# Weighted sums of two key tiles back to back in every second period of an attention pipeline

## The reference

```
attn = einsum('bhld,bhrd->bhlr', q, k) * 0.25
rel  = einsum('bhld,lrd->bhlr', q, dist_emb[clip(r - l, -64, 8) + 64]) * 0.25
attn = softmax(attn + rel, axis=-1)
out  = einsum('bhlr,bhrd->bhld', attn, v)
```

## Time and profile before

| | |
|---|---|
| median of 3 runs | 1690.88 us |
| the profiled execution | 1693.59 us |
| its span | 1691.8 us |
| TensorE matmul busy over the span | 1395.4 us (82%) |
| VectorE busy | 1091.4 us (65%) |
| ScalarE busy | 991.8 us (59%) |
| GpSimd busy | 235.3 us (14%) |

### The profile page before, as it was taken

How to read it: one execution, slowest core, us unless ns; L and a number is a source line. 1 busy time by engine, 2 the same in 40 slices (tenths; PEclk the granted TensorE clock), 3 DMA queues, 4 the chain that set the end, 5 groups by cost and what they waited for, 6 DMA issues and landing times. The chain is left out here.

```text
span 1691.8 us, 25838 instructions
## 1 busy us (share of the span) xinstructions
PE 1395.4 (82%) x8108; PEld 685.2 (41%) x8108; DVE 1091.4 (65%) x2552; ACT 991.8 (59%) x1697; POOL 235.3 (14%) x472
## 2 busy tenths in 40 slices
PE   7851599999999999999999997798995989810487
PEld 4520133444334443344433432566662434300476
DVE  3540888878888788887888870246432329979554
ACT  4530177777777777777777775244443548868600
POOL 0001121212212122121221200113310000000011
PEclk9975599999999999999999998878867999965699
DMA  6859588787887878878788611322202102205022
GB/s 191 237 151 243 167 222 233 198 231 220 223 233 196 231 220 224 233 196 234 216 226 232 176 53 54 111 71 66 61 26 87 37 0 112 112 26 195 27 85 89
DMA packets 263819, 260.03 MB, mean 154 GB/s; under 512 B 65902, under 2 KB 250894, under 8 KB 259598
## 3 DMA queue, kind: packets, MB, share of 16 engines
q1 hardware_dynamic: 263694, 258.49, 53.2%
HBM read 149.30 MB, written 108.35 MB: 152 GB/s over the span
## 5 line engine op out<-in xcount | busy, mean ns | idle before, releaser
L500 ACT ACTIVATE pr<-scoresT 128x512 f32<-128x512 f32 x1024 | 550.5, 600 | 217.3 <-PE scoresT L744 158.9
L740 PE MATMUL scoresT<-qT,kT 99*128 99x512 bf16 (+7 forms) x1408 | 358.9, 326 | 6.7 <-issue 5.0
L609 DVE CUSTOM_DVE_ANT_0 junk<-scores_for_max,win 128x200 f32<-128x200 f32 (+2 forms) x512 | 180.1, 352 | 199.3 <-PE scores_for_max L715 196.7
L614 DVE TENSOR_REDUCE mx<-scores_for_max 128x1 f32<-128x888 f32 (+6 forms) x448 | 301.7, 673 | 0.0
L612 DVE TENSOR_REDUCE mx<-scores_for_max 128x1 f32<-128x64 f32 (+6 forms) x448 | 277.5, 619 | 0.0
L757 PE MATMUL attn_out<-pr,vS 128*17 128x512 f32 x2048 | 269.4, 598 | 0.1
L740 PEld LDWEIGHTS scoresT<-qT,kT 99*128 99x128 bf16 (+1 forms) x1408 | 113.7, 97 | 335.4 <-ACT rows L480 97.8
L744 PE MATMUL scoresT<-idf,win 128*128 128x128 f32 x1024 | 218.2, 274 | 0.0
L714 PE MATMUL scores_for_max<-kX,qT 64*128 64x512 bf16 x512 | 169.7, 394 | 19.4 <-DVE mx L614 18.0
L1741 PE MATMUL banks<-w_downT,work 128*128 128x256 f32 x384 | 88.5, 395 | 105.8 <-DVE work L1712 105.8
L715 PE MATMUL scores_for_max<-kX,qX 64*128 64x512 bf16 x512 | 169.8, 394 | 0.0
(11 more groups left out here) (161 smaller groups left out, 1691.9 us busy)
## 6 DMA issues: line engine op xcount, KB each, us to landing
rel_table<-rows SPq DMA_DIRECT2D x128, 512.0 KB, 4.1
win<-rel_table SPq DMA_DIRECT2D x128, 512.0 KB, 5.3
up_raw<-ub SPq DMA_DIRECT2D x6, 1536.0 KB, 5.1
ub<-up_raw SPq DMA_DIRECT2D x6, 1536.0 KB, 6.3
qT<-q_parts SPq DMA_DIRECT2D x32, 256.0 KB, 7.4
kX<-k_parts SPq DMA_DIRECT2D x64, 128.0 KB, 4.9
kT<-k_parts SPq DMA_DIRECT2D x32, 256.0 KB, 5.4
q_parts<-part SPq DMA_DIRECT2D x32, 192.0 KB, 4.3
```

The costliest lines, as they stand in the source:

```text
L500: nc.scalar.activation(pr[:, n % NPR, h, :], bank, ACT.Exp).then_inc(t_read, 1)
L609: last = nc.vector.tensor_tensor_reduce(junk[:, n % 2, 0:z - a], bank[:, a:z], win[:, T % NW, q4, h, u:u + z - a], 1.0, NEG, ALU.add, ALU. ...
L614: last = nc.vector.tensor_reduce(mx[:, T % 2, q4, h, 2:3], bank[:, z:L], AX.X, ALU.max)
L740: last = mm(bank[:, a:e], k[0:r], q[0:r, a:e], start=(n == 0), stop=not near and n == len(pieces) - 1, skip_group_check=True)
```

## The change

In place of one `weigh` in each period, TensorE does none in odd periods and two in even ones: those of the two key tiles before. Nothing else is moved, no buffer is added, and no other engine's program changes.

```
                     if kt == SHIFT_AT and T + 1 < NT:
                         turn_shift(T + 1)
-                    if kt:
+                    if kt and kt % 2 == 0:
+                        weigh(T, kt - 2)
                         weigh(T, kt - 1)
-                    elif T:
+                    elif kt == 0 and T:
+                        weigh(T - 1, TL - 2)
                         weigh(T - 1, TL - 1)
+            weigh(NT - 1, TL - 2)
             weigh(NT - 1, TL - 1)
             turn_out(NT - 1)
```

## The result

The change makes the kernel slower. Its median is 1747.2 us (4 runs, 1741.05 to 1756.81), against 1691.98 us for the kernel before on the same chip (4 runs). The ratio is 1.0326, with a 95% interval of 1.0265 to 1.0388. The forecast was 1752 us, range 1739 to 1773, with TensorE held up by VectorE's chunk buffers.

A forecast was written before the change was run, and what follows sets the result against it. TensorE was taken to be held up by VectorE's two-deep chunk buffers: 121 pairs at 0.51 us, 61.9, less 1.2 for the last 6, gave +60.7 us. On 1690.9 that is 1752 us, range 1739 to 1773.

The forecast's parts named there:

- The floor: Two-deep chunk buffers: VectorE allows no less than 3.24 us from one period's first chunk to the next's second, 3.11 outer.
- odd stretches: From an odd period's first chunk to the even period's second; six at 3.24 and two at 3.11, 25.66 us.
- The pair: Two `weigh` in a row in each even period; the second was taken to add 0.88 us, its passes alone.
- The saved changes: TensorE's switches between `weigh` and other matmuls; a pair of periods was to have 0.20 us less work.
- The rival of two full changes: The second `weigh` still pays both changes, 1.08 us in place of 0.88; 1777 us in all, chance 0.08.
- The sum: Sixteen periods: odd and even parts together 56.99 us against 52.90, so 4.09 us more for 8 pairs, 0.51 a pair.
- even stretches: From an even period's second chunk to the next odd first chunk; eight grow by 0.88 each, 24.29 to 31.33 us.
- VectorE recovers part: Waits in even periods vanish as VectorE and ScalarE catch up; loss 12 us smaller, 1740, within the forecast's 0.75.
- The last pairs: The 6 pairs at the end, after the chunks stop, only gain 0.20 us each: -1.2 us.
- the two dearer rivals: Two `weigh` in a row paying both changes, 1777 us, and ScalarE later by 0.2 us a pair, 1776; chances 0.08 and 0.06.
- narrowly in period 1: ScalarE's three score banks let the second chunk come at 2.6 or 3.1 us, hidden under VectorE's 3.24.
- a third chunk buffer: Would make true the rival that TensorE alone sets the pace: 25 us faster, 1666, chance 0.05.

The follow-up runs named there:

- pairs_act: The changed kernel with ScalarE's exponentials covering 256 of 512 queries from the fourth period on; median 1738.83 us, against 1682.36 us for the order of before with this cut.
- pairs_dve: The changed kernel with each VectorE maximum reduction beside the window reading at most 64 columns; median 1678.09 us.
- single_dve: The kernel before, its order kept, with each VectorE maximum reduction beside the window reading at most 64 columns; median 1664.24 us.
- pairs_both: The changed kernel with VectorE's reductions at most 64 columns wide and half of ScalarE's exponentials left out from the fourth period on; median 1642.3 us.

## Why the prediction was right

**The floor.** Forecast 3.24 us between an odd period's first chunk and the next second chunk, and 3.11 in outer query tiles; measured 3.24 and 3.11 in 118 of 121 odd stretches. Cutting VectorE's work took seven tenths of the loss away (61.2 to 17.6 us), and cutting ScalarE's too turned the rest into a gain of 5.7 us, which shows that this is the cause and not only a coincidence of numbers.

**The pair.** Forecast 0.88 us for the second `weigh`, measured 0.87 in the stretch shown. The saved changes are 1.43 us per 16 periods; eight times 0.20, 1.6, was the estimate. The rival of two full changes is refuted by the pass starts. The prediction said that the trace of before has no two in a row. It has one such pair, the last two `weigh` of the stage:

```profile
1042.87 2.09 PE L757 MATMUL attn_out<-pr,vS 128*17 128x512 f32 x16
```

It would not have settled the price, as its second `weigh` also waits for its last exponential: that one ends at 1043.85, and the `weigh` starts at 1043.91.

**The sum.** Forecast 4.09 us more per 16 periods, measured 3.75. The odd stretches were right; the even ones were forecast at 31.33 us, which leaves 31.0 measured. In two of the eight even stretches a wait of before went away, as the small rival "VectorE recovers part" had it (in the one from 643.29 to 645.88 it was the small job's wait for a bank): they grew by 0.71 and 0.78 us in place of 0.87, 0.25 us in all. The rest is 0.87 for a second `weigh` where 0.88 was taken. Over the stage up to the last chunk the loss is 58.4 us in place of 61.9.

The last pairs were wrong in sign: each was to gain 0.20 us, 1.2 in all, as no chunks are left there, and the stretch became 2.8 us longer. 1.5 us of that are the pair at the lower clock; the rest is ScalarE's, as the runs with its work cut show. The prediction had ScalarE only under VectorE's floor and did not ask what it does where that floor is gone. So the whole stage, 61.2 us against 60.7 forecast, agrees better than its parts do, and that much is luck. The median moved by 55.2 us, to 1747 in place of 1752; between the two lies mostly the scatter of what is beside the stage, of which more below. The range held this, but it did not reach the two dearer rivals (1776 and 1777), although the prediction says that it takes in most of them: it ends at 1773.

**ScalarE.** The prediction placed it just under VectorE's floor, "narrowly in period 1". That was right as to the order of the two, and pairs_act shows it. But one sentence was wrong: that with VectorE out of the way (a third chunk buffer) the pairs would win their 25 us. pairs_dve, where VectorE is out of the way by another means, has a stage 17.6 us longer than its yardstick's; a third buffer itself was not tried. The estimate at hand said so already: ScalarE's chain put the second chunk at 2.6 or 3.1 us, and TensorE's own work in most of these stretches is shorter than that, so below VectorE's floor comes ScalarE's, not TensorE's work.

## What to carry to other kernels

An engine at 99% busy is not alone in setting the pace if another at 81% reads its output through a ring of two buffers: before work is grouped on the first, work out the shortest distance between two fillings of the same buffer, and compare it with the shortest stretch that the new order makes. Average slack (0.3 us a period here) did not show it; grouping moved 1.08 us out of one period into the next. And when one floor is taken away, ask for the next one: the saving counts only down to there.

## What the runs showed that I had not expected

Within the profiled execution of the kernel before, the cycles of 16 periods agree within 52.89 to 52.94 us, leaving out the first and the last. Outside the stage the executions scatter far more: what is left of the span beside it was 851.7 us in the kernel before, 849.1 in the changed one, and 836.2 to 844.8 us in the five experiments that touch nothing there. In the four with VectorE's work cut it was 819.2 to 833.9 us, but there the cut acts too, on the 24 chunks ahead of the stage: from the first chunk to the first scores single_dve took 22.5 us where the kernel before took 35.3. Against that scatter, more than the 5.7 us that pairs_both gained in its stage, the length of the touched stage tells small changes apart where the whole time does not. It must start and end at work that the change leaves in its place: taken from the first `weigh`, which the change itself moves, pairs_both would seem to gain 8.8 us and the change to cost 57.6.

TensorE's changes of kind cost the same in all directions seen: about 0.1 us into or out of the weighted sums, into or out of the chunks, and from a chunk straight into a `weigh`. So each group of chunks put directly beside a `weigh` saves about 0.1 us.
